# A graph network of attention and sum passes: each engine loads a step's registers in that step, not a whole turn's at the loop's turn

## What is computed

```python
# attention (once in the first layer, three times in the third)
alpha = leaky_relu(al_s[src] + al_d[dst] + al_e, 0.2)
ex    = exp(alpha - segment_max(alpha, dst)[dst])
out   = segment_sum(h[src] * (ex / segment_sum(ex, dst)[dst])[:, None], dst)
# second layer: sums by source, then a small network
edge_aggr = zeros(n, 128).at[src].add(edge_attr_128)
# fourth layer, five rounds: h + segment_sum(h[src], dst), then matrices and batch norms
```

## Time and profile before

| | us |
|---|---|
| median of three runs | 10009.14 (9993.36 to 10016.74) |
| span of the profiled execution | 8265.9 |
| sums by source | 430.7, from 1328.0 |
| stream pass | 681.8, from 1921.9 |
| three counting passes | 1122.3, 1121.1, 1121.2, from 2846.0, 4034.7, 5223.0 |

### The profile page before, as it was taken

One profiled execution on the slowest core, in us unless ns is written; L12 is line 12 of the kernel. 1 busy time (PEld: TensorE's weight loads), 2 busy tenths in 40 slices (PEclk: granted clock), 3 DMA queues, 4 the chain that ended last, 5 costly groups with the idle time before them and its releaser, 6 DMA issues. The chain is left out here.

```text
span 8265.9 us, 141750 instructions
## 1 busy us (share of the span) xinstructions
PE 5352.1 (65%) x31293; PEld 4178.9 (51%) x31294; DVE 4566.5 (55%) x12677; ACT 4612.0 (56%) x9736; POOL 4195.4 (51%) x4209
## 2 busy tenths in 40 slices
PE   3211214735886477777567777577776789898996
PEld 2100004735775255555455555455554668686775
DVE  3400003546887677777577777677777454545445
ACT  1188882005775377777567776577765344434444
POOL 1777776775663277777377775577774000000000
PEclk9655556867998799999799999799998899999998
DMA  3333335854552166666366665466663567585674
GB/s 83 101 104 106 104 105 163 225 149 137 134 135 80 44 143 144 143 145 144 97 143 144 143 145 126 116 144 144 144 144 88 187 220 262 193 272 186 213 254 144
DMA packets 867526, 1219.30 MB, mean 148 GB/s; under 512 B 132976, under 2 KB 713386, under 8 KB 866388
## 3 DMA queue, kind: packets, MB, share of 16 engines
q1 hardware_dynamic: 350948, 583.84, 22.7%
q0 software_dynamic: 134144, 280.83, 16.5%
q10 hardware_dynamic: 381744, 348.10, 14.8%
HBM read 908.23 MB, written 306.54 MB: 147 GB/s over the span
## 5 line engine op out<-in xcount | busy, mean ns | idle before, releaser
L1233 POOL DMA_INDIRECT ring<-gat_rows,src_idx x2496 | 2473.3, 991 | 1044.3 <-issue 1043.1
L1889 PE MATMUL ps<-wide,features 128*128 128x504 f32 (+1 forms) x6370 | 1435.2, 384 | 15.1 <-DVE features L1789 15.1
L1453 PE MATMUL ps<-ring,xT_b 128*128 x8192 | 1202.7, 293 | 260.1 <-ACT xT_b L1545 247.4
L1505 DVE CUSTOM_DVE_ANT_0 xT_a<-ps,rows_mask,xT_a 128x512 f32<-128x512 f32 x1024 | 768.4, 750 | 1014.4 <-issue 760.0
L1889 PEld LDWEIGHTS ps<-wide,features 128*128 128x128 f32 x6370 | 1155.7, 189 | 246.5 <-DVE wide L1757 16.1
L1453 PEld LDWEIGHTS ps<-ring,xT_b 128*128 128x128 f32 x8192 | 1081.2, 205 | 328.7 <-issue 327.1
L1429 ACT ACTIVATE al_cols<-ps 128x504 f16<-128x504 f32 x1536 | 823.2, 588 | 590.2 <-issue 517.3
L1418 PE MATMUL ps<-al_cols,w_static 128*128 128x504 f16 x1536 | 622.4, 405 | 697.4 <-ACT al_cols L1429 561.9
L1537 ACT ACTIVATE xT_a<-xT_a,state 128x514 f32<-128x514 f32 x1024 | 742.6, 725 | 587.5 <-DVE xT_a L1505 409.3
L711 POOL DMA_INDIRECT by_src<-ring,state x832 | 803.5, 966 | 255.9 <-issue 253.0
L1083 POOL TENSOR_TENSOR x_nodes<-x_nodes,last_state 128x1280 f32<-128x1280 f32 x3 | 9.9, 3312 | 1786.4 <-SPq L242 1786.4
(11 more groups left out here) (401 smaller groups left out, 8417.4 us busy)
## 6 DMA issues: line engine op xcount, KB each, us to landing
counts<-al_cols ACTq DMA_DIRECT2D x1536, 126.0 KB
xT_a<-counts SPq DMA_DIRECT2D x245, 756.0 KB, 4.3
rows_mask<-dloc_rows ACTq DMA_DIRECT2D x1052, 128.0 KB
xT_b<-counts SPq DMA_DIRECT2D x150, 812.0 KB
xT_a<-counts SPq DMA_DIRECT2D x95, 812.0 KB
ring<-by_src SPq DMA_DIRECT2D x52, 1040.0 KB, 6.7
ring<-in_edge_attr SPq DMA_DIRECT2D x103, 512.0 KB, 4.5
ring<-gat_rows,src_idx POOLq DMA_INDIRECT x2912
```

The costliest lines, as they stand in the source:

```text
L1233: pool.indirect_dma_start(ring[:, o:o + RC], None, table[:, :], bass.IndirectOffsetOnAxis(src_idx[:, t * W + u:t * W + u + 1], 0)).then_in ...
L1453: m = pe.matmul(bank(BO + v % 2, R), pw[v % 4][:, w * P:(w + 1) * P], ring[:, w * RC:][:, bass.ds(look(SLOT, u - 7), R)], start=w == 0, st ...
L1505: dve.tensor_tensor_reduce(out=m[:, 0:TE], in0=spread(u)[:, 0:TE], in1=mask[u % 4], scale=1.0, scalar=m[:, TE + 1:TE + 2], op0=ALU.add, op ...
L1889: m = pe.matmul(bank_of(w), H2[:, (i * 2 + x) * D:(i * 2 + x + 1) * D], wide[n % 2][:, o:o + width_of(w)], start=i == 0 and x == 0, stop=F ...
```

## The change

The three row tables become one table per engine, interleaved by step and shifted so that one entry holds all that a step of that engine looks up: `pe_table` (SLOT of step n-7), `dve_table` (SLOT of n+3, BC of n+1, BC of n-8), `act_table` (BC of n, NEED of n+3). `pipeline` loads one entry per step (three registers on VectorE, two on ScalarE), and on TensorE the entries of four steps at every fourth step. VectorE's work ahead of the first step moves to `dve_first`, with three loads of its own. The sums use the same pipeline with turns of 16 steps: four registers per step on VectorE, four per fourth step on TensorE. Values that a semaphore is waited against get `max(value, 1)` in place of a snap. What the setup does for the tables changes with them.

```diff
-SU = 8
+SU = 16
+        PE_ROWS = [(SLOT, -PE_LAG)]
+        DVE_ROWS = [(SLOT, AHEAD), (BC, 1), (BC, -DVE_LAG)]
+        ACT_ROWS = [(BC, 0), (NEED, AHEAD)]
...
-        s(dve, lambda: dve.memset(steptab[:, :], 0))
...
+        s.together((dve, lambda: dve.memset(act_tab[:, :], 0)), (dve, lambda: dve.memset(dve_tab[:, :], 0)),
+                   (dve, lambda: dve.memset(pe_tab[:, :], 0)))
+        s(dve, lambda: dve.memset(of_row(act_tab, 2, 1), T))
+        s.together(*[(dve, lambda t=t, c=c, i=i, r=r, lead=lead: dve.tensor_copy(
...
+        def counts_of(eng, regs):
+            to = count_regs[eng.engine][0:len(regs)]
+            for x, y in zip(to, regs):
+                eng.reg_alu(x, y, 1, ALU.max)
+            return to
...
-                for tab, first, count, rows in tables:
-                    regs = registers(used, tab, base * len(rows) + first, count)
...
+            def values(at, rows):
+                raw = regs[0:len(rows)]
+                eng.load(raw, table[0:1, bass.ds(at * rows_each, len(rows))])
+                return [counts_of(eng, [x])[0] if r == NEED else
+                        eng.snap(x, min_val=LIMIT[r][0], max_val=LIMIT[r][1]) for x, (r, _) in zip(raw, rows)]
...
                 for u in us:
+                    if u % every == 0:
+                        found = values(base + u + AHEAD, rows * every)
+                    now = dict(zip(rows, found[u % every * rows_each:(u % every + 1) * rows_each]))
...
-            pipeline(pe, pe_body, 7, [step_row(SLOT, 8)])
-            pipeline(dve, dve_body, 8, [step_row(BC, 8, 4), step_row(SLOT, 0, 4)])
-            pipeline(act, act_body, 6, [(act_tab, 0, 2 * U, [(BC, 0), (NEED, -AHEAD)])])
+            pipeline(pe, pe_body, PE_LAG, pe_tab, PE_ROWS, 4)
+            pipeline(dve, dve_body, DVE_LAG, dve_tab, DVE_ROWS, 1, dve_first)
+            pipeline(act, act_body, ACT_LAG, act_tab, ACT_ROWS, 1)
...
-            pipeline(pe, pe_body, 0, [], U=SU, K=K2, side_by_side=[(tab(0)[:, U:], [SLOT])])
-            pipeline(dve, dve_body, 2, [], U=SU, K=K2, side_by_side=[(by_four, [NODE, COL, NEED, BLOCK])])
+            pipeline(pe, pe_body, 0, tab(0)[:, U - AHEAD:], [(SLOT, 0)], 4, U=SU, K=K2)
+            pipeline(dve, dve_body, 2, by_four, sum_rows, 1, U=SU, K=K2)
```

More of the change, by code:

```diff
@@ L54 @@
 AHEAD = 3
+PE_LAG, DVE_LAG, ACT_LAG = 7, 8, 6
 SOON = 3
+assert KT >= AHEAD + DVE_LAG + K
 FIRST = 14
@@ L785, in source_steps @@
             for i in range(4):
-                late = 2 if i == 3 else 0
+                late = AHEAD + (2 if i == 3 else 0)
                 s(dve, lambda: dve.tensor_copy(
@@ L1199, in build @@
         step_regs = {e.engine: [e.alloc_register(f"step{i}") for i in range(n)]
-                     for e, n in ((dve, 3 * U), (act, 3 * U), (pe, 3 * U), (sp, U))}
+                     for e, n in ((dve, U), (act, 3 * U), (pe, 3 * U), (sp, U))}
+        count_regs = {e.engine: [e.alloc_register(f"count{i}") for i in range(n)]
+                      for e, n in ((dve, 2), (act, 2), (sp, U))}
+        def counts_of(eng, regs):
[3 more added lines that the diff above has]
+            return to
         def fetch(table):
@@ L1320, in build @@
                  BLOCK: (FS, NB * C + FS)}
[L1322 to L1337, removed]
-            def part(base, us, begin, end):
-                found, used = {}, 0
-                for tab, first, count, rows in tables:
-                    regs = registers(used, tab, base * len(rows) + first, count)
[L1343 to L1354, removed]
-                for u in us:
@@ new lines, in pipeline, with look @@
+        def pipeline(eng, body, lag, table, rows, every, first=None, U=U, K=K):
+            regs = step_regs[eng.engine]
+            def values(at, rows):
[3 more added lines that the diff above has]
+                        eng.snap(x, min_val=LIMIT[r][0], max_val=LIMIT[r][1]) for x, (r, _) in zip(raw, rows)]
+            def part(base, us, begin, end):
+                found = []
+                for u in us:
+                    if u % every == 0:
+                        found = values(base + u + AHEAD, rows * every)
+                    now = dict(zip(rows, found[u % every * rows_each:(u % every + 1) * rows_each]))
+                    def look(r, lead, now=now):
+                        return now[r, lead]
@@ L1357, in part @@
                     body(base + u, u, lambda d, u=u: (u >= d if begin else d > u if end else True), look)
+            rows_each = len(rows)
+            if first is not None:
+                first([values(i, rows)[0] for i in range(AHEAD)])
             part(0, range(U), True, False)
@@ L1527, in dve_body, with dve_first @@
                         make_nodes(n + 1, (u + 1) % U, lambda d: have(d - 1))
+            def dve_first(slots):
+                make_mask(0, 0)
+                make_mask(1, 1)
+                if not streamed:
+                    make_nodes(0, 0, lambda d: d == 0)
+                for i, slot in enumerate(slots):
+                    scores(i, i, slot)
+                dve.tensor_scalar(sm[0][:, TE + 1:TE + 2], S[:, MAX:MAX + 1], 1.0, None, ALU.mult
+                                  ).then_inc(q["old_max"], 1)
             def act_body(n, u, have, look):
@@ L1605, in source_sums @@
                 sp.load(seen, fr[0:1, g:g + 1])
-                load(g, g % RG, sp.snap(seen[0], min_val=1, max_val=K2))
+                load(g, g % RG, counts_of(sp, seen)[0])
                 while kept_now < pairs and (kept_now + 1) * (loads - RG - 4) <= (g - RG - 2) * pairs:
@@ L1631, in dve_body @@
                 if have(0):
-                    dve.wait_ge(q["stage"], look(NEED, u))
+                    dve.wait_ge(q["stage"], look(NEED, 0))
                     if have(4):
```

64 lines of the change are left out of this document (31 added, 33 removed).

## The result

The changed kernel took 10070.15 us (median of eight runs, 10042.36 to 10105.66) against 10017.97 us for the kernel before on the same chip: ratio 1.0047, 95% interval 1.0026 to 1.0067. It is 0.47% slower, a little over the 0.2% that can be told from no change, where 1.2% faster was forecast; 10070 lies above the range of 9840 to 9965.

The account below looks back on a forecast made before the run. GpSimd's issuing was taken to bound the counting passes and, with SyncE's load/store order, the sums; compute the stream pass. Terms -75-39-8+1.5 = -120.5 us took 10009.1 to 9888.6, stated as 9887, range 9840 to 9965.

Parts of the forecast that it names:

- The base of the sum: Run time against trace span: the 1743.2 us beyond the 8265.9 us span belong to no changed stage and stay.
- the last of the prediction's own signs of being wrong: Counting passes: the prediction is wrong if POOL begins to wait for room there.
- The price of a small load: Register loads per step: 63 ns a register on VectorE; three registers 0.28 us, two 0.19, TensorE's four some 0.35.
- What hides it: Engine queues run 0.75 to 1.0 us ahead of the work, so 0.5 us per step goes into that.
- slower rival: VectorE's queue: small loads not hidden, 0.5 to 0.55 us between engine steps; total +280 us, 10289; chance 0.10.
- Stream pass: Its 15 turns each lose 5.5 us, -82, and TensorE's loads and waits cost +7: -75 us, so 607 us.
- the 2.35 us: VectorE's plain step in the stream pass: above this, small loads show and the prediction is wrong.
- Counting passes: A turn gets 4.1 us shorter, compute catches up with GpSimd: -13.1 us in each of three, -39.
- Sums: Sums stage: sooner steps shrink only the 23.6 us wait for a stored buffer: -8 us, bounds 0 and -20.
- The refetch: Stream pass turn: an instruction refetch adds 3.4 us at VectorE's branch; total -55 us, 9954; chance 0.24.
- Nothing comes of it: Stream and counting passes: half of a load shows, 0.25 us per step; total 9994 us; chance 0.05.
- the last rival: Whole run: time beyond the span shrinks in proportion, so -120.5 us becomes -146, 9863; chance 0.11.

Follow-up runs that it names:

- turn_loads_2: The kernel before with max(value, 1) in place of bounded values at semaphore waits, run on the slower kind of chip: 10001.28 us, ratio 0.9998.
- changed_again: The changed kernel as it is, run again on the faster kind of chip: 8271.33 us against 8269.64 for the kernel before, ratio 1.0002.
- aligned: The changed kernel with four-word loads at multiples of 16 bytes on VectorE, ScalarE and TensorE: 8149.25 us, ratio 0.9856 (faster chip); 10031.65 us, 1.0019 (slower chip).
- turn_loads: The kernel before with max(value, 1) in place of bounded values at semaphore waits, on the faster kind of chip: 8272.99 us, ratio 1.0006.
- every_fourth: The changed kernel with aligned loads of 12, 8 and 4 registers at every fourth step: 10009.42 us, 0.9997 (slower chip); 8177.78 us, 0.9885 (faster chip).
- tensor_aligned: The changed kernel with only TensorE's table shifted by one word, aligning its loads of four: 10067.39 us, ratio 1.006, on the slower chip; again 10069 us, 1.0057.

## Why the prediction was wrong

**The base of the sum: wrong.** "The 1743.2 us beyond the span belong to no stage that changes" is the first step that failed. The time is in the stages: on chip A, where the result was measured, a counting pass of the kernel before takes 1438 us and not 1122, its stream pass 993 and not 682. POOL, which never waits for room in the earlier trace rows, waits for it in the first counting pass, in the kernel before (turn_loads_2) and in the changed one:

```profile
L1244 POOL DMA_INDIRECT ring<-gat_rows,src_idx x832 | 829.3, 997 | 603.0 <-SPq L1220 330.3 <-issue 272.7
```

```profile
L1255 POOL DMA_INDIRECT ring<-gat_rows,src_idx x832 | 826.3, 993 | 641.0 <-SPq L1229 363.7 <-issue 277.3
```

So "GpSimd's issuing sets this pass" is true on chip B only, and the last of the prediction's own signs of being wrong came. What came back and what was lost differ with it: 66 us (sums and stream pass) against 52 in the profiles on B, 14 against 85 in those on A, and the ratios are 1.0002 and 1.0047.

**The price of a small load: wrong, on both chips.** The 63 ns a register came from the bulk loads, whose tables begin at a multiple of 16 bytes, and the supporting row, ScalarE's four registers at 0.31 us, is such a one as well. Measured: 0.746, 0.50 (0.67 in the counting passes) and 1.00 us, with 0.34, 0.31 and 0.33 where four words stand aligned. The first row that spoke against it, SyncE's 16 registers in 3.27 us, was in the earlier trace rows: it reads its table from entry 16 it - 13, 12 bytes past a multiple of 16. No run moved that table, but I had taken the row for a difference of engines, and on VectorE, ScalarE and TensorE the difference was one of addresses. The Trainium skill (Runtime: NRT & Kernel Launch, Instruction fetch mechanics) has about 200 ns a register, also in bulk; the unaligned loads are near it (214 to 259 ns in all but ScalarE's in the counting passes), the aligned ones aren't (60 to 86). The register loads of that page come from HBM, those of this kernel from SBUF.

**What hides it: half right.** VectorE's cover holds most of its load: of 0.40 us saved per step, 0.04 showed in the stream pass (633 against 644 us). What failed is the cover elsewhere. In counting passes ScalarE's queue has three DMA issues of some 0.35 us in each step and a load of its own in every second, and 262 loads of 0.67 us came before L1550. The prediction had "ScalarE's load of 0.31 us has room in its step already" as a reason against its slower rival, and no row of what else stands in that queue.

**Stream pass: right in mechanism.** From one maximum to the next the step at the turn took 6.37 us in the median and takes 2.91 in changed_again, 2.45 in aligned, and the mean granted clock of the pass rises from 0.94 to 0.98. With the price forecast, that is in aligned, the pass is 600 us against 607; with the real price 644. There the steps with TensorE's load take 2.5 to 2.6 us and the others 2.3 to 2.4, about the 2.35 us that the prediction had named as a sign of loads that show.

**Counting passes: right with the forecast price, not with the real one.** Aligned gives 22 us in all and not 39: compute catches up (in the first pass the last maximum starts 14.8 us behind the last gather, 26.3 in turn_loads), but the gathers themselves take longer, 1089 us from first to last against 1079, at a mean of 1.004 us against 0.993. With the real price the three are 52 us slower.

**Sums: right, larger than forecast.** 28 us on chip B, not 8, and beyond the bound of 20; the wait for the stored buffer fell from 25 to 12 us and the gathers' own time by 13. Setup: +3 us, not +1.5.

For chip B the forecast of -120.5 us is met by the aligned kernel (span 8150.1 against 8273.8, -123.7), but in part by luck: the stream pass gave 82 us and not 75, the counting passes 22 and not 39, the sums 26 and not 8, and the rest cost 7 and not 1.5. The term that was mis-sized is the small load, by 2.6 times on VectorE and up to 3.5 on ScalarE, and the base was another chip's. On chip A no gain came even with the load at the price forecast: aligned has 1.0019 there.

**The rivals.** The refetch didn't come (0.3 us at the branch with 285 instructions). The slower rival named the right mechanism, small loads that aren't hidden, but put it on VectorE, where it is mostly hidden, and priced it at +280; it was ScalarE's, and the counting passes lost 52 us by the profiles on chip B and some 85 on A. "Nothing comes of it" has the total of chip B, not the way there: gains of 66 us against that loss. Time beyond the span, which the last rival would have shrunk, there was none.

**What stays open.** Why chip A stretches the passes that gather; long register instructions, waits for an event without a sender and longer passes go together in the counting passes, but the first are missing in two stages that stretch as well. That register loads make the changed kernel slower on A is shown by every_fourth, at 0.9997 (up to 1.0011), against tensor_aligned's 1.006 (from 1.0038) on the same chip. That it is ScalarE's among them is only argued from the order of ratios: 1.0047, 1.006 and 1.0057 with its loads as changed, 1.002, 1.0019 and 0.9997 with aligned ones; but for every_fourth the intervals overlap or touch.

The best version is aligned: 1.4% faster than before on chip B, the same as before on A within its interval.

## What to carry to other kernels

Before loads are split into small ones, look where each begins and ends: here a register load that began at a multiple of 16 bytes and took whole groups of four words cost 0.25 us a group, and every other one cost about as much for each single word. So pad an entry to four words and shift the table until the index of the first is a multiple of four. Then ask of each engine's queue, not of its busy time, what stands behind the load; here the queue with three DMA issues a step was the tight one, and in the stream pass one long hold cost more than several short ones. And where a trace's span and the run's time differ, find out which of the two the stages belong to before a sum is made.

## What the hardware showed that I had not expected

- A load's price by address: four words 0.344 us aligned, 0.965 us one word off; 24 words 5.39 us off, where 28 aligned ones take 1.85. Three words on VectorE take 0.74 to 0.76 us in the median wherever they begin.
- Two places to run, with 8.27 and 10.01 ms for one program, the busy time of VectorE in a pass the same within 2.5%; on the slower one ScalarE's register instructions of 29 ns take up to 0.74 us now and then, and a gain of 1.4% vanishes.
- Gathers of the same size took 0.989 to 0.993 us in the mean of a counting pass of turn_loads and 0.991 to 1.012 in the variants with aligned loads; what makes the difference was not tried.
